# Pair features folded into dense rows, W1's feature rows by plain transfers, and the splitting of W1 re-ordered, in a recommender's two-layer network

## The reference, cut to what matters

```
cont_emb = emb_table[:13][None, :, :] * conts[:, :, None]
cate_emb = emb_table[cates]
cc = jnp.concatenate([cont_emb, cate_emb], axis=1)
gram = jnp.einsum('bfd,bgd->bfg', cc, cc)
pairs = gram[:, ROWS, COLS]                       # the 741 pairs i < j
X = jnp.concatenate([cont_emb.reshape(B, -1), cate_emb.reshape(B, -1), pairs], axis=1)
X = jax.nn.relu(_layernorm(X @ W1 + b1, ln1_g, ln1_b))
X = jax.nn.relu(_layernorm(X @ W2 + b2, ln2_g, ln2_b))
logit = jax.nn.sigmoid(X @ Wout + bout)
```

## Time and profile before

| what | value |
|---|---|
| median of 3 runs | 835.93 us (834.75 to 836.88) |
| the profiled execution | 834.96 us, its span 833.2 us |
| PE busy | 777.5 us, 93% of the span |
| DVE, ACT, POOL busy | 480.8, 500.7, 512.6 us |
| granted TensorE clock, mean | 0.969 |
| DMA moved | 50.64 MB, mean 61 GB/s |

### The profile page before, as it was taken

How to read it: one execution, slowest core, us unless ns; L and a number is a source line. 1 busy time by engine, 2 the same in 40 slices (tenths; PEclk the granted TensorE clock), 3 DMA queues, 4 the chain that set the end, 5 groups by cost and what they waited for, 6 DMA issues and landing times.

```text
span 833.2 us, 11377 instructions
## 1 busy us (share of the span) xinstructions
PE 777.5 (93%) x3775; PEld 639.0 (77%) x3775; DVE 480.8 (58%) x954; ACT 500.7 (60%) x831; POOL 512.6 (62%) x456
## 2 busy tenths in 40 slices
PE   6567789999999999999999999999999999999994
PEld 1346667888888888888888888888877888888883
DVE  2446364646556465564655546555466665655665
ACT  0455755775867758677586775867766554445441
POOL 5776177777777777777777777777400244344433
PEclk9868998999999999999999999999999999999998
DMA  9999238768585675856758567585754211111000
GB/s 264 169 161 60 59 64 29 47 30 50 27 49 48 27 48 25 50 48 26 48 26 50 47 27 48 26 50 48 98 198 151 76 51 28 48 50 50 25 1 0
DMA packets 28076, 50.64 MB, mean 61 GB/s; under 512 B 12269, under 2 KB 12525, under 8 KB 28055
## 3 DMA queue, kind: packets, MB, share of 16 engines
q0 software_dynamic: 15536, 15.33, 42.8%
q1 hardware_dynamic: 9783, 26.32, 10.1%
q10 hardware_dynamic: 2736, 8.71, 2.6%
HBM read 41.93 MB, written 8.40 MB: 60 GB/s over the span
## 4 chain that ended last, share of the span: by engine, by line
PE 92%; DVE 4%; ACT 3%; issue 1%; DMA 0%; ACTq 0%; DVEq 0%
PE acc L494 25%; PE acc L495 24%; PE acc L496 24%; PE tr L536 5%; PE gr L573 3%; PE tr L573 3%; PE tr L519 2%; PE acc L589 2%; PE gr L519 1%; PE tr L671 1%; PE gr L671 1%; DVE w_lo L997 1%; PE tr L545 1%; PE gr L552 1%; ACT w_hi L807 0%
## 5 line engine op out<-in xcount | busy, mean ns | idle before, releaser
L457 POOL DMA_INDIRECT xb<-in_L_rec_emb_table,idx x416 | 434.7, 1045 | 131.5 <-issue 126.0
L494 PE MATMUL acc<-w_hi,x_hl 128*128 128x512 f32 x416 | 176.3, 424 | 25.0 <-DVE w_lo L997 18.9
L495 PE MATMUL acc<-w_lo,x_hl 128*128 128x512 f32 x416 | 167.2, 402 | 0.0
L496 PE MATMUL acc<-w_hi,x_hl 128*128 128x512 f32 x416 | 166.8, 401 | 0.0
L477 POOL TENSOR_TENSOR raw_lo<-raw_lo,raw_hi 128x1024 f32<-128x1024 f32 x15 | 35.9, 2392 | 154.5 <-ACT raw_lo L892 154.5
L743 ACT CAST g_move<-x_hl 64x384 fp32r<-64x384 f32 (+1 forms) x192 | 125.6, 654 | 2.2
L494 PEld LDWEIGHTS acc<-w_hi,x_hl 128*128 128x128 f32 x416 | 81.0, 195 | 46.1 <-DVE w_lo L997 19.8
L494 PE MATMUL acc<-w_hi 128*128 128x512 f32 x256 | 101.1, 395 | 1.4 <-DVE raw_lo L1183 1.4
L740 ACT CAST g_still<-x_hl 64x384 fp32r<-64x384 f32 (+1 forms) x96 | 99.8, 1039 | 2.1
L496 PE MATMUL acc<-w_hi,w_lo 128*128 128x512 f32 x256 | 99.7, 390 | 0.0
L495 PE MATMUL acc<-w_lo,w_hi 128*128 128x512 f32 x256 | 99.7, 390 | 0.0
(11 more groups left out here) (111 smaller groups left out, 1180.1 us busy)
## 6 DMA issues: line engine op xcount, KB each, us to landing
raw_lo<-in_L_rec_W SPq DMA_DIRECT2D x21, 512.0 KB, 9.5
h_scratch<-h_row ACTq DMA_DIRECT2D x16, 512.0 KB, 5.4
raw_hi<-h_scratch SPq DMA_DIRECT2D x16, 512.0 KB, 3.6
xb<-in_L_rec_emb_table,idx POOLq DMA_INDIRECT x416, 5.8
raw_hi<-in_L_rec_W SPq DMA_DIRECT2D x6, 512.0 KB, 6.7
raw_lo<-in_L_rec_W SPq DMA_DIRECT2D x10, 104.0 KB
raw_hi<-in_L_rec_b SPq DMA_DIRECT2D x1, 512.0 KB, 3.8
raw_hi<-in_L_rec_ln_g SPq DMA_DIRECT2D x1, 512.0 KB, 4.8
```

Of the source, the lines that this page charges most:

```text
L457: nc.gpsimd.indirect_dma_start(out=xb[:, f * DIM:(f + 1) * DIM], out_offset=None, in_=emb, in_offset=bass.IndirectOffsetOnAxis(ap=idx[:, p ...
L494: nc.tensor.matmul(o, a, w, start=first, stop=False)
L495: nc.tensor.matmul(o, a, v, start=False, stop=False)
L496: return nc.tensor.matmul(o, b, w, start=False, stop=last)
```

## The change

- **Folded features.** The 325 categorical pairs are laid out as 13 rows ("folds") of 25: fold s holds the pairs (s, s+1 .. 25) and (25 - s, 26 - s .. 25). Consecutive pairs of a field stay together, so that their rows of W1 are consecutive runs. DVE writes the sum of the two halves in three small operations directly into `chosen`, which now lies in `dots`; the 26 x 26 sum and ACT's copy `choose_pairs` are gone. `take_dots` waits for `l_trans` in place of `chosen_done`, and `norm1` for `chosen_done` in place of `l_trans`. The 78 continuous pairs are folded alike, by three operations in place of one in every tile, and by three in place of twelve in the setup.
- **Feature rows of W1.** All 741 rows come by 53 plain transfers on SP (`row_pieces`: 12 for k-tile 13 beside its two continuous-times-categorical ones, 25 categorical pieces of 1 to 25 rows beside the other 14), sorted by k-tile, behind a wait for the last embedding k-tile; then b1. By k-tile 13 to 18 they are 14, 6, 6, 8, 9 and 10. POOL keeps one small indirect transfer, of four rows that meet zeros.
- **Order of the splits.** k-tiles 0 to 3 are split before ACT waits for V (`split 0`), 4 to 6 after group 0, 7 and 8 before group 2, 9 before copies 1, 10 before group 3, 11 before copies 2, 12 before the dots. In tile 1: 13 and 14 before group 2, 15 and 16 before copies 1, 17 and 18 before copies 2. PE's order `SECOND` follows.
- **Indices.** Tile 0's 26 columns get their own chain of four operations, ahead of the other 390 columns'.
- **vbd** has memory of its own, and DVE waits no longer for the product of V before `ee_bc`.

The diff, cut:

```diff
-SECOND = (0, 1, 2, "factor prev", 3, "late prev", "own 1", 4, 5, 6, "own 2", 7, 8, "own 3", 9, "cont", 10,
-          13, 14, 15, 16, 17, 18, "gram 0", 11, "gram 1", "gram 2", "gram 3", "next 0", 12)
+FIRST = (0, 1, 2, 3, "own 1", 4, 5, 6, "own 2", 7, 8, 9, "own 3", 10, "cont", 11,
+         "gram 0", "gram 1", "gram 2", "gram 3", 12, "next 0")
+SECOND = (0, 1, 2, "factor prev", 3, "late prev", "own 1", 4, 5, 6, "own 2", 13, 7, 14, 8, 15, 9, "own 3", 16, 17, 18,
+          "cont", 10, "gram 0", 11, "gram 1", "gram 2", "gram 3", "next 0", 12)
...
-W1_BEFORE = {"own 1": (0, 1, 2, 3), "own 2": (4, 5, 6), "own 3": (7, 8, 9), "copies": (10,), "dots": (11, 12),
-             "norm": (13, 14, 15, 16, 17, 18)}
+W1_FIRST = {"split 0": (0, 1, 2, 3), "split 1": (4, 5, 6), "split 2": (7, 8), "copies 1": (9,), "split 3": (10,),
+            "copies 2": (11,), "dots": (12,)}
+W1_SECOND = {"split 2": (13, 14), "copies 1": (15, 16), "copies 2": (17, 18)}
...
+def cate_pieces():
+
+    pieces = []
+    for s in range(FOLDS):
+        if s < 5:
+            tile, at = FT + 1, FOLD * s
+        elif s < 10:
+            tile, at = FT + 2, FOLD * (s - 5)
+        else:
+            tile, at = FT, PART_PAD + FOLD * (s - 10)
+        pieces.append((tile, at + s, FOLD - s, pair_row(CONT + s, CONT + s + 1)))
+        if s > 0:
+            pieces.append((tile, at, s, pair_row(CONT + FOLD - s, CONT + CATE - s)))
+    return pieces
+
+
+def row_pieces():
+
+    return sorted(nn_pieces() + cc_pieces() + cate_pieces(), key=lambda piece: piece[0])
...
-            for s, at_row, n, row in cc_pieces():
-                sp.dma_start(raw_lo[EK + s][at_row:at_row + n, :], W1[row:row + n, :]).then_inc(w1_cc[s], 16)
+            sp.wait_ge(w1_in[EK - 1], 16)
+            for s, at_row, n, row in row_pieces():
+                sp.dma_start(raw_lo[EK + s][at_row:at_row + n, :], W1[row:row + n, :]).then_inc(w1_rows[s], 16)
             sp.dma_start(raw_lo[EK + FT][PART - 1:PART, :], b1.unsqueeze(0)).then_inc(b1_in, 16)
             sp.wait_ge(acc_ready, 2)
...
-            pool.wait_ge(rows_in, 16)
             gather(0, 0, first=True)
             gather(1, 1)
-            for s in (0, FT, FT + 1, FT + 2):
-                feature_rows_of(s)
+            pool.wait_ge(rows_in, 16)
+            rows_under_zeros()
...
-            def choose_pairs(x):
-
-                act.wait_ge(sums_done, x + 1)
-                if not isinstance(x, int) or x >= 1:
-                    act.wait_ge(l_trans, x)
-                view = sums[:, :]
-                diags = bass.AP(view.tensor, view.offset + 1, [view.ap[0], [1, DIAGS], [CATE + 1, DIAG]])
-                nc.scalar.copy(chosen[:, :].rearrange("p (k f) -> p k f", f=DIAG), diags).then_inc(chosen_done, 1)
...
-                        act.wait_ge(chosen_done, x)
+                        act.wait_ge(l_trans, x)
...
-                if k not in (EK + 1, EK + 2):
+                if k < EK:
                     act.wait_ge(w1_in[k], 16)
-                if EK <= k <= EK + FT:
-                    act.wait_ge(w1_cc[k - EK], 16 * sum(p[0] == k - EK for p in cc_pieces()))
+                else:
+                    act.wait_ge(w1_rows[k - EK], 16 * sum(p[0] == k - EK for p in row_pieces()))
                 if k == EK + FT:
+                    act.wait_ge(w1_pad, 16)
                     act.wait_ge(b1_in, 16)
                     act.wait_ge(v_in, 1)
                 m = rows_of(k)
                 nc.scalar.copy(w1_hi[0:m, k, :], raw_lo[k][0:m, :]).then_inc(w1_rounded, 1)
...
+            w1_before("split 0")
             act.wait_ge(v_done, 1)
             nc.scalar.copy(raw_lo[EK + FT][V_AT:V_AT + CONT, :],
                            acc[1][0:CONT, :, :].rearrange("p h n -> p (h n)")).then_inc(v_in, 1)
             split_group(0, 0)
-            w1_before("own 1")
+            w1_before("split 1")
             split_group(0, 1)
             act.wait_ge(setup_done, 1)
             gram_copies(0, 0)
 
             def iteration(x, par, first=False, last=False):
 
+                table = W1_FIRST if first else W1_SECOND if isinstance(x, int) and x == 1 else None
+                if table:
+                    w1_before("split 2", table)
+                split_group(x, 2)
+                if table:
+                    w1_before("copies 1", table)
+                gram_copies(x, 1)
                 if first:
-                    w1_before("own 2")
-                split_group(x, 2)
-                if first:
-                    w1_before("own 3")
-                gram_copies(x, 1)
+                    w1_before("split 3")
                 split_group(x, 3)
-                if first:
-                    w1_before("copies")
+                if table:
+                    w1_before("copies 2", table)
                 gram_copies(x, 2)
                 if first:
                     w1_before("dots")
                 else:
-                    if isinstance(x, int) and x == 1:
-                        w1_before("norm")
                     norm1(x - 1, 1 - par)
...
+            index_chain(0, 0, CATE, idx[:, 0, :], idx_done)
+            index_chain(3, CATE, TILES * CATE, idx_all[:, CATE:TILES * CATE])
             indices(1, 1)
             step(nc.vector.memset(to_zero, 0.0))
+            step(nc.vector.memset(vbd[:, :, :], 0.0))
...
-            dve.wait_ge(v_done, 1)
             dve.wait_ge(setup, done[0])
             nc.vector.tensor_copy(ee_bc[:, :], tr[:, 1, 0:NN])
...
-                nn = feats[:, NN_AT:NN_AT + NN].rearrange("p (k i) -> p k i", i=CONT)
-                view = c2[:, :, :]
-                shifted = bass.AP(view.tensor, view.offset + 1, [view.ap[0], [1, CONT // 2], [1, CONT]])
-                TT(nn, c2[:, 0:1, :].to_broadcast([P, CONT // 2, CONT]), shifted, ALU.mult).then_inc(nn_step, 1)
-                dve.wait_ge(nn_step, x + 1)
+                nn, c = feats[:, NN_AT:NN_AT + NN], c1[:, :]
+                TT(nn_upper(nn), *nn_upper_of(c), ALU.mult).then_inc(nn_step, 1)
+                dve.wait_ge(nn_step, 3 * x + 1)
+                TT(nn_lower(nn), *nn_lower_of(c), ALU.mult).then_inc(nn_step, 1)
+                dve.wait_ge(nn_step, 3 * x + 2)
+                TT(nn_right(nn), *nn_right_of(c), ALU.mult).then_inc(nn_step, 1)
+                dve.wait_ge(nn_step, 3 * x + 3)
                 TT(feats[:, NN_AT:NN_AT + NN], feats[:, NN_AT:NN_AT + NN], ee_bc[:, :], ALU.mult)
...
-                whole = pairs[:, :, 0:CATE]
-                TT(sums[:, :].rearrange("p (g f) -> p g f", f=CATE), whole, whole.rearrange("p g f -> p f g"),
-                   ALU.add).then_inc(sums_done, 1)
+                S = pairs[:, :, :]
+                TT(spread(chosen, 0, (FOLD + 1, SIDE), (1, SIDE)),
+                   spread(S, 1, (QUAD + 1, SIDE), (1, SIDE)),
+                   spread(S, QUAD, (QUAD + 1, SIDE), (QUAD, SIDE)), ALU.add).then_inc(sides_done, 1)
+                dve.wait_ge(sides_done, 2 * x + 1)
+                TT(spread(chosen, FOLD + 1 - SIDE, (FOLD + 1, SIDE), (1, SIDE)),
+                   spread(S, QUAD * (FOLD - 1) + SIDE + 2, (-QUAD, SIDE), (1, SIDE)),
+                   spread(S, QUAD * (SIDE + 2) + FOLD - 1, (-1, SIDE), (QUAD, SIDE)), ALU.add).then_inc(sides_done, 1)
+                dve.wait_ge(sides_done, 2 * x + 2)
+                TT(spread(chosen, SIDE, (FOLD, FOLDS), (1, FOLDS)),
+                   spread(S, FOLDS, (QUAD, FOLDS), (1, FOLDS)),
+                   spread(S, QUAD * FOLDS, (1, FOLDS), (QUAD, FOLDS)), ALU.add).then_inc(chosen_done, 1)
```

More of the change, by code:

```diff
@@ L583, in _, with v_product @@
             nc.tensor.matmul(tr[:, 1, 0:NN], ones, ee, start=True, stop=True).then_inc(s_ready, 1)
[L585 removed]
+            def v_product(n):
                 pe.wait_ge(v_rows_in[n], 16)
@@ L1106, in norm1, with w1_before @@
                    ALU.subtract, ALU.mult).then_inc(norm_dve, 1)
-            def w1_before(what):
-                for k in W1_BEFORE[what]:
+            def w1_before(what, table=W1_FIRST):
+                for k in table[what]:
                     w1_lo_part(k)
             cont_features(0, first=True)
+            w1_before("split 0")
             split_group(0, 0)
-            w1_before("own 1")
+            w1_before("split 1")
             split_group(0, 1)
@@ L1120, in iteration @@
             def iteration(x, par, first=False, last=False):
-                if first:
-                    w1_before("own 2")
-                split_group(x, 2)
-                if first:
-                    w1_before("own 3")
-                gram_copies(x, 1)
+                table = W1_FIRST if first else W1_SECOND if isinstance(x, int) and x == 1 else None
+                if table:
+                    w1_before("split 2", table)
+                split_group(x, 2)
+                if table:
+                    w1_before("copies 1", table)
+                gram_copies(x, 1)
+                if first:
+                    w1_before("split 3")
                 split_group(x, 3)
```

150 lines of the change are left out of this document (79 added, 71 removed).

## The result

The changed kernel's median is 852.67 us over four runs (850.37 to 854.61), against 835.89 for the kernel before in the same session: a ratio of 1.022, 95% interval [1.018, 1.025]. It is slower by 16.8 us, the forecast was 857.0. The profiled execution took 850.37 us, its span is 848.6 us, 15.4 more than before.

A forecast was written before the change was run, and what follows sets the result against it. PE bounds the steady tiles and second layer, so only the start and tile 15's end can change: 834.96 + 22.9 - 1.2 = 856.7, median 1.0 above the profiled run, forecast 857 us; range 830 to 872.

The forecast's parts named there:

- next 0: Transpose of tile 2's first group, made during tile 1; the tick for the start, 127.43 us before, forecast 150.3.
- k-tiles 0 and 4: Tile 0 on PE: k-tile 0 starts at about 29.8 us, 2 us later; k-tile 4 at about 42.2 instead of 47.0.
- Tile 1 without a wait for rows: Tile 1 if W1's rows came in time: tile 2's first transposes at about 120 us, 7.5 us sooner than 127.43.
- T: Landing of the last feature row of W1 (b1, last of 54 issues): taken as 124 us, between 120 and 128.
- by rows: Estimate of the row transfers priced by row count: 47 us of issues, ending at 109, last landing at 120 us.
- by pieces: Estimate of the row transfers priced by number: 54 at 1.33 us, faster after 121 us, last landing about 128 us.
- rival 2: Rows land near the break-even, at 95 to 112 us, if the fast stretch lasts: 829 to 845 us; chance 0.14.
- Rival 3: Odd-sized pieces' rows go one behind the other on one engine: last landing about 134 us, 867 us total; chance 0.14.
- The chain behind T: Tile 1, from the last row's landing through ACT, PE and DVE to tile 2's first transposes: 26.3 us.
- The break-even: Landing time of the last row from which the wait shows against the old kernel: 102 us.
- Steady tiles: Later tiles: ACT and DVE have time to spare, 0 change; at most 0.3 x 13 tiles = 4 us if overrun.
- Tile 15's end: PE's 1.68 us wait at 620.17 us for sum and copy: these become about 1.0 us, 1.2 us saved.

The follow-up runs named there:

- b1_first: The changed kernel with b1's transfer issued ahead of the 53 pieces, on chip A: 1007.1 us, 0.988 of the kernel before.
- even_cuts_c: The changed kernel with pieces of 17, 19, 21, 23 and 25 rows cut into 16 and the rest, later session on chip B: 998.6 us, 0.974 of before.
- idx_first: The kernel before with tile 0's own index chain first and nothing else of the change, on chip A: 1040.0 us, 1.018 of before.

## Why the prediction was right

**What bounds the kernel.** The start, and there "next 0" of tile 1. The loss, 18.8 us, had all come in by then; the steady tiles added nothing and the end gave 3.2 back.

**The indices' chain.** The first gather starts at 5.16 in place of 6.30, the one us that was forecast; it bought nothing.

**k-tiles 0 and 4: wrong in size.** Forecast 29.8 and 42.2; measured 35.74 and 48.04 against 27.71 and 47.00 before. The mechanism is as told: ACT rounds k-tile 3 when it has landed and PE starts 3.5 us later (32.19 + 3.55 = 35.74; told was 26.5 + 3.3). The term that failed is that W1 would land as before: k-tile 3 was in at 32.2 and not at 26.5, k-tile 8 at 51.9 and not 46.3, k-tile 12 at 67.7 and not at 62 (61.0 before). The step between k-tiles is the same 3.95 us; the whole row of them is 5.6 to 6.7 us late, from the fifth transfer of V's blocks on (15.2 against 12.2). Why is open: it isn't the index chain (above), and the same kernel order had k-tile 3 at 26 to 31 on the other chips.

**Tile 1 without a wait for rows: wrong by the same.** ACT was told to want k-tiles 13 and 14 at 89 and was there at 96.67, and its split of tile 1's group 0 came at 78.89, 0.8 us before the old kernel's 79.66, where PE at 71 had been told (the prediction's "next 0" of tile 1 near 71 is these transposes of tile 1's first group; measured 78.25). So the 7.5 us that the new order was to bring were 1.1: ACT, not waiting, would have begun k-tile 16 at 99.99 and "next 0" would have been at 126.3 against 127.43. As forecast, this error cost nothing, since ACT only arrived at the wait at another time.

**T, the term that decides: right in sum, wrong in its parts.** Forecast 124 (120 to 128), measured 119.98. The forecast had the issues last until 109 to 121 and more, at 1.33 us each or by rows, and over 50 us in all; the landing was told 11 us behind the last one by rows, and 1 to 4 us by pieces (44 by 121, ten more at 0.33 to 0.6, T = 128). Measured: 32.1 us of issues at 0.61 us, which the prediction had named as a sign of being wrong, done at 100.3; and a landing 19.5 us behind the last one. Had the pieces landed 3.6 us behind their issue, as the cut ones did, T would have been 104 and the change, by this estimate, within some 3 us of before: rival 2. The error of the first part and the error of the second nearly cancel, and that is luck. The price by pieces came from 16 issues that stood behind four full k-tiles in flight, and that was no price for pieces alone. That a piece costs a gather's turn of 1.25 us, as was told, is not borne out by 0.61.

**Rival 3 was the mechanism of the lag.** In the changed kernel k-tile 16's rows land at 96.3, k-tile 17's at 107.8 and 18's at 119.6, and of these two k-tiles the pieces have 25, 24, 23, 22, 21 and 20, 19, 18, 17, 16 rows. All 53 are issued by 99.9. The queues' view of 100 to 120 us (packets, MB, share of the 16 engines) shows what is left of SP's queue:

```profile
q0 software_dynamic: 457, 0.45, 63.3%
q1 hardware_dynamic: 141, 0.39, 5.6%
```

5.6% of 16 engines over 20 us is 17.9 us of one engine's time: what remained for 20 us was about as much work as a single engine can do in them. The cuts took the lag from 12.0 (b1_first) to 3.6 us on one chip and from 14.3 to 4.8 on the other. So that the odd long pieces cause it is shown by two pairs, one trace each. A lag alone would not show it: before, with no such piece among the 16, b1 landed 11.7 us behind its issue, but then q1 had 10.5% of the engines' time in 69 to 80 us. The Trainium skill has the rule in "DMA: Bandwidth & Descriptors", section "Why a DMA increments its semaphore by 16 and not by 1": the largest number up to 16 that divides the rows, and on this kind of queue the lowest-numbered engines, so that 23, 19 and 17 rows would all queue on one and the same engine. The trace agrees twice. The 5.6% are one engine's worth.

And the number of engines can be counted in the trace's semaphore updates. Each full k-tile's transfer gives its semaphore 16 of them. If a piece gives one for each engine that the rule names, and one more where that is fewer than 16, the pieces of k-tiles 13 to 18 give 117, 71, 72, 102, 55 and 81, and b1's row, on one engine, 2. The changed kernel's trace has exactly these seven counts, and the kernel before's has the 27, 71, 72 and 21 of its 16 pieces, so that the rule could have been tested ahead of the forecast. So b1's row is a single-engine transfer behind all the others: it landed 0.2 us behind k-tile 18's last row. By the rule the first engine has 39 of k-tile 17's 125 rows and 46 of 18's, and 14 and 14 once they are cut; the 46 took the 11.8 us from 107.8 to 119.6, 0.26 us a row. The rule would have given the sign and about the time (867 by the prediction's own price of 0.5 us a row, about twice the measured one); I gave it 0.14.

**The chain behind T.** T + 26.3 was told: measured 119.98 to 146.24, 26.3. PE had k-tile 17 at T + 7.2 (told 7.3; the terms listed for it add up to 8.1, but the second of the "two parts 2.0" isn't ahead of it), ACT's first dots came at 140.92, T + 20.9 (told 15.8 + 4.5 = 20.3), and "next 0" 5.3 behind them (told 6.0). It held within 1.1 us in all the runs of the table, and within 2.0 in the other six. The forecast of 150.3 is off by the 4.0 us of T and nothing else.

**The break-even.** Told: T = 102. By the rows of the changed kernel it is 127.43 - 26.3 = 101.1 on the first chip. On chip B ACT isn't at k-tile 16 before 109 to 112, which is why the rows are in time there.

**Steady tiles: right.** Told 0, at most 4; measured 34.85 in place of 34.80 us a tile, and tile 15 no later than tile 2. The first of the continuous pairs' three operations of 0.20 and the product behind them, in DVE's timeline, with PE's k-tile 4 of the same tile:

```profile
401.30 0.20 DVE L1061 TENSOR_TENSOR feats<-c 128x36 f32<-128x36 f32 x1
...
402.00 0.30 DVE L1067 TENSOR_TENSOR feats<-feats,ee_bc 128x78 f32<-128x78 f32 x1
402.22 0.54 DVE L1031 TENSOR_TENSOR x_hl<-gr,x_hl 128x384 fp32r<-128x384 f32 x1
...
403.03 0.40 PE L510 MATMUL acc<-w_hi,x_hl 128*128 128x512 f32 x1
```

The split ends at 402.76, 0.27 us before PE wants it; there were 0.74. The room was nearly used up, as told.

**Tile 15's end: right in kind.** Told -1.2, measured -3.2. PE's wait went from 1.68 to 0.86 and 0.4 us beside it are gone: 1.2. Of the other 2.0, the clock has 1.4 to 1.5: before, PE's granted clock is 0.94 in 600 to 624 us, at the lower of its two levels for 3.4 us from 620.94 on, and the eight transposes behind the wait take 1.97 us; after, it is 1.00 in 618 to 642 and they take 1.09. These are 0.9 us, and the first k-tiles behind them have the rest: PE is 17.2 us later than before at these transposes and 15.8 later at the next eight. Some 0.4 us are won behind PE's last product; from what is open. Ahead of the fall in the kernel before stands the wait of 1.68 us, ahead of no fall in the changed one the wait of 0.86; that the one causes the other wasn't tested. The prediction priced only the wait.

**The sum.** Told 22.9 - 1.2 = 21.7, measured 18.8 - 0.2 - 3.2 = 15.4: 4.1 for T, 0.2 for the tiles, 2.0 for the end. The forecast's own last step is 0.7 off too: 856.7 and the 1.0 between profiled run and median make 857.7, not 857.

## What to carry to other kernels

A wait that an engine meets in its order is priced by the arrival of the last thing behind it, so put the last row of a long list of small transfers where its consumer is last, or wait for it last: here b1's 4 KB, last of 54, held copies, splits and the norm that needed none of it, though k-tile 16's other rows had been in for 23.5 us. What that is worth in time is not shown: on chip A, with b1 first, ACT came behind all the rows. Count a list of plain transfers by issue and by landing apart: the issues went at 0.4 to 0.8 us, and what came late was the tail of pieces with awkward row counts; cutting 17, 19, 21, 23 and 25 rows into 16 and a rest added five issues and brought the last landing forward by 8 us. And walk the chain behind such a wait once, with the durations of the profile: it was the one part of this forecast that held within 2 us in eleven of twelve traces.

## What the runs showed of the hardware that was not expected

**Chips on which a tile takes 47.5 us.** On chips A and B every tile has, around the grams, a stand of PE, ACT and DVE together. PE and ACT in a steady tile of even_cuts_c (timelines), then its waits of 400 to 500 us in total, times, longest:

```profile
446.59 1.10 PE L597 MATMUL gr<-g_move,g_still 128*128 128x104 f32 x8 [0.24 <-issue]
...
451.33 0.40 PE L520 MATMUL acc<-w_hi,x_hl 128*128 128x512 f32 x1
457.99 1.95 PE L597 MATMUL gr<-g_move,g_still 128*128 128x104 f32 x8 [6.26 <-ACT dots L798]
459.74 1.91 PE L597 MATMUL tr<-g_move,g_still 128*128 128x104 f32 x8
```

```profile
456.91 1.03 ACT L798 ACTIVATE dots<-gr 32x208 f32<-32x208 f32 x2 [8.14 <-remote]
```

```profile
ACT dots L798 <- remote: 16.3, 2, 8.1
...
PE gr L597 <- ACT dots L798: 12.5, 2, 6.3
```

ACT and DVE wait 7 to 8 us a tile for a release that the trace calls remote, though gram 0, which gives it, is recorded as ended at 447.69, 9.2 us before 456.91, and PE then waits for them. PE's granted clock is 1.00 in 448 to 457 us and 0.50 in 457.9 to 462, and the grams behind the stand take 1.95 in place of 1.10 us. The tiles are as long in the old index order and with whole or cut pieces, and the kernel before runs at 1028 to 1042 us there too; what the cause is stays open.

**The sign of a change can differ by chip.** With before's rows and orders (idx_first), "next 0" shows up in ACT's split at 152.5 us on chip A and its tiles take 49.1 us on the mean; with the change it is at 136 to 140 and 47.5 in the three traces of that chip. So a changed kernel seems to win there in the start and in the tiles; that rests on one trace of the older kind, and on none of the kernel before itself. The changed kernel's time is 0.979 of before on chip B, and 1.022 on the chip of the forecast. A forecast made from one chip's trace is a forecast for such chips.

**One list of issues, three prices.** One and the same list of 53 pieces took 0.38, 0.59 to 0.62 and 0.79 us an issue: started at 84 us, at 62 to 68, and at 49 while embedding k-tiles were still in flight. The median issue took 0.30 to 0.40 us in each; what differs is a few issues, of up to 0.9 us in the first case and 2.3 to 3.0 in the others. Why those take long wasn't tested.
